# Two heads of the mLSTM scores per TensorE step, gates on 68 rows, and all orders set anew, in a one-core decoder layer

## The reference

```
x = layernorm(x + attention(x))          # 16 heads of 16, score bias by distance, softmax, output projection
x = layernorm(x + mlstm(x, ctx, ctx))    # 4 heads of 64, queries from x, keys and values from ctx
x = layernorm(x + ffn(x))                # 256 -> 1024 (gate, up) -> 256, rows quantised to 8 bits, ternary weights

# mlstm, for each head
ig, fg = concat(x, ctx, ctx) @ gate kernels + biases       # one number per row and head
cs     = cumsum(log_sigmoid(fg));  log_D = cs_i - cs_j + ig_j   (j <= i)
D      = exp(log_D - rowmax(log_D))
C      = (q k^T / 8) * D
h      = C v / (max(|rowsum C|, exp(-rowmax)) + 1e-6), then a norm over each head
```

## Time and profile before

| | us |
|---|---|
| median of 3 executions | 827.5 (827.5 to 833.78) |
| the profiled execution | 828.54 |
| its span, first to last instruction | 826.8 |
| TensorE busy | 698.1 |
| VectorE busy | 640.6 |
| ScalarE busy | 626.0 |
| GpSimd busy | 491.1 |

### The profile page before, as it was taken

How to read it: one execution, slowest core, us unless ns; L and a number is a source line. 1 busy time by engine, 2 the same in 40 slices (tenths; PEclk the granted TensorE clock), 3 DMA queues, 4 the chain that set the end, 5 groups by cost and what they waited for, 6 DMA issues and landing times.

```text
span 826.8 us, 17709 instructions
## 1 busy us (share of the span) xinstructions
PE 698.1 (84%) x5138; PEld 519.6 (63%) x5168; DVE 640.6 (77%) x2437; ACT 626.0 (76%) x1284; POOL 491.1 (59%) x833
## 2 busy tenths in 40 slices
PE   4279888899898989898989898999989898975642
PEld 3257657577675858585858676777758575743411
DVE  3745454888988888888888988988888889876743
ACT  0427674979898988888888989898989888885622
POOL 2536453657677676776675757676776763735232
PEclk8679996999999999999999999999999999989866
DMA  8876734080605060513224160707060601010100
GB/s 257 152 135 78 94 64 79 2 140 2 143 12 141 15 140 15 119 37 95 61 56 100 35 120 4 152 2 146 10 141 14 123 20 53 14 52 14 39 14 13
DMA packets 63177, 59.97 MB, mean 73 GB/s; under 512 B 6437, under 2 KB 62826, under 8 KB 63082
## 3 DMA queue, kind: packets, MB, share of 16 engines
q1 hardware_dynamic: 63082, 58.84, 34.6%
HBM read 29.39 MB, written 4.26 MB: 41 GB/s over the span
## 4 chain that ended last, share of the span: by engine, by line
PE 69%; ACT 8%; DVE 7%; issue 6%; POOL 5%; DMA 3%; SPq 2%; POOLq 0%; DVEq 0%; ACTq 0%
PE pT L604 12%; PE pO L621 8%; PE pC L661 6%; PE pS L588 6%; PE pC L637 3%; PE pA L747 3%; PE pA L637 3%; PE pC L708 2%; PE pB L708 2%; PE pB L574 2%; SPq L296 2%; ACT L1114 2%; PE pA L695 2%; PE pB L757 1%; PE pC L725 1%
## 5 line engine op out<-in xcount | busy, mean ns | idle before, releaser
L1299 DVE CUSTOM_DVE_ANT_0 sc<-pS,bias 128x256 f32<-128x256 f32 x512 | 200.6, 417 | 39.9 <-PE pS L588 37.6
L604 PE MATMUL pT<-ident,sc 128*128 128x128 f32 x1024 | 155.9, 285 | 35.5 <-ACT pr L946 33.1
L946 ACT ACTIVATE pr<-pT 128x512 f32<-128x512 f32 x256 | 149.0, 596 | 19.2 <-PE pT L604 18.8
L604 PEld LDWEIGHTS pT<-ident,sc 128*128 128x128 f32 x1024 | 123.0, 146 | 59.7 <-issue 52.4
L426 POOL TENSOR_SCALAR sc<-sc,mx 128x256 f32<-128x256 f32 x256 | 122.3, 483 | 59.4 <-DVE mx L1299 56.3
L934 ACT ACTIVATE sc<-sc,mx 128x256 f32<-128x256 f32 x256 | 127.8, 512 | 1.1 <-DVE mx L1299 0.9
L588 PE MATMUL pS<-ks,qs 96*128 96x256 bf16 x512 | 97.5, 278 | 5.5 <-DVE mx L1299 5.5
L478 POOL TENSOR_SCALAR_AFFINE_SELECT mb<-mb 128x256 f32<-128x256 f32 x64 | 26.2, 409 | 98.7 <-ACT mb L973 94.2
L621 PE MATMUL pO<-pr,va 128*32 128x256 f32 x1024 | 76.5, 421 | 0.0
L438 POOL TENSOR_SCALAR hq<-h 128x512 bf16<-128x512 f32 x64 | 38.5, 619 | 55.1 <-ACT h L1122 55.1
L588 PEld LDWEIGHTS pS<-ks,qs 96*128 96x128 bf16 x512 | 44.9, 99 | 37.9 <-DVE mx L1299 12.5
(11 more groups left out here) (236 smaller groups left out, 1790.0 us busy)
## 6 DMA issues: line engine op xcount, KB each, us to landing
qs<-parts SPq DMA_DIRECT2D x96, 128.0 KB, 5.4
ks<-parts SPq DMA_DIRECT2D x96, 128.0 KB, 6.3
mb<-mrows SPq DMA_DIRECT2D x16, 512.0 KB, 6.7
xin<-in_x SPq DMA_DIRECT2D x16, 256.0 KB, 2.8
bias<-in_L_attn_pos_bias SPq DMA_DIRECT2D x4, 1024.0 KB, 21.2
xb<-in_x SPq DMA_DIRECT2D x16, 256.0 KB, 7.0
cx<-in_ctx SPq DMA_DIRECT2D x32, 128.0 KB, 2.2
out<-hq SPq DMA_DIRECT2D x16, 256.0 KB, 5.8
```

What stands on the lines that cost most here:

```text
L604: ins = pe.transpose(bank[:, kt * S + t * P:kt * S + t * P + P], sc[:, s % RING, t, kt * P:kt * P + P], ident[:])
L946: act.activation(flat(pr[:, s % RING, :, :]), pT[s % 2][:, :], ACT.Exp, scale=-1.0)\
L1299: dve.tensor_tensor_reduce(out=sc[:, s % RING, t, :], in0=pS[s % 2][:, t * S:t * S + S], in1=bias[:, t, s, ::-1], scale=1.0, scalar=LOW, o ...
```

## The change

1. `mem_scores` takes a pair of heads instead of one. It leases two banks at once, then issues the wide product of head 2*pair (partitions 0 to 63) and of head 2*pair+1 (partitions 64 to 127), then both narrow products in the same turn. There are two such steps for a batch where there were four.
2. The forget gates move from row and column 32 to 64: `gate_w` has 68 columns, `gate_b`, `gt`, `sp` and `am` 68 rows. The gates' products write 68 rows, the exponents are turned with 68 rows.
3. The bodies of all five queues, and the table `uses`, are written in a new order. No step is added or dropped except that four `mem_scores` became two.

The core of the difference:

```diff
-        gate_w = sb("gate_w", [P, 6, 64])
-        gate_b = sb("gate_b", [64, 1])
+        gate_w = sb("gate_w", [P, 6, 64 + XH])
+        gate_b = sb("gate_b", [64 + XH, 1])
...
         uses = [
-            ("cv1", 2, cv_sb, 2), ("qk3", 2, c_sb, 4), ("cv2", 2, cv_sb, 3), ("ott0", 1, att_v, 3),
...
+            ("u1", 3, h_v, 4), ("g2", 3, h_v, 5), ("u2", 3, h_v, 6), ("g3", 3, h_v, 7), ("am", 2, am_a, 2),
+            ("u3", 3, h_v, 8), ("qk0", 2, c_sb, 1), ("qk1", 2, c_sb, 2), ("cv0", 2, cv_sb, 1), ("cv1", 2, cv_sb, 2),
+            ("qk2", 2, c_sb, 3), ("qk3", 2, c_sb, 4), ("cv2", 2, cv_sb, 3), ("ott0", 1, att_v, 3),
...
+            ("k", -2, k_f, 1), ("xqT", 2, xq_sb, 1), ("g0", 2, h_v, 1), ("u0", 2, h_v, 2), ("g1", 2, h_v, 3),
         ]
...
-            def mem_scores(c, hh):
+            def mem_scores(c, pair):
...
-                bank = lease(pe, f"qk{hh}", c)
-                if hh == 0:
+                banks = [lease(pe, f"qk{2 * pair + i}", c) for i in range(2)]
+                if pair == 0:
                     pe.wait_ge(x1T_sb.sem, x1T_sb.at(c, 1))
                     pe.wait_ge(cxT_sb.sem, cxT_sb.at(c, 1))
-                r = slice(64 * (hh % 2), 64 * (hh % 2) + 64)
-                pe.matmul(bank[:, 0:S], cxT[r, hh // 2, 0:P], x1T[r, hh // 2, :], start=True, stop=True)
-                pe.matmul(bank[:, S:S + P], cxT[r, hh // 2, P:S], x1T[r, hh // 2, P:S], start=True, stop=True)\
-                    .then_inc(qk_ps.sem, 1)
+                for i in range(2):
+                    r = slice(64 * i, 64 * i + 64)
+                    pe.matmul(banks[i][:, 0:S], cxT[r, pair, 0:P], x1T[r, pair, :], start=True, stop=True)
+                for i in range(2):
+                    r = slice(64 * i, 64 * i + 64)
+                    pe.matmul(banks[i][:, S:S + P], cxT[r, pair, P:S], x1T[r, pair, P:S], start=True, stop=True)\
+                        .then_inc(qk_ps.sem, 1)
...
-                    pe.matmul(bank[0:64, 0:S], gate_w[:, 2 + kt, :], cxT[:, kt, :], start=(kt == 0), stop=False)
+                    pe.matmul(bank[0:64 + XH, 0:S], gate_w[:, 2 + kt, :], cxT[:, kt, :], start=(kt == 0), stop=False)
...
-                    ins = pe.transpose(bank[:, t * P:t * P + 64], am[:, t * P:t * P + P], ident[0:64, 0:64])
+                    ins = pe.transpose(bank[:, t * P:t * P + 64 + XH], am[:, t * P:t * P + P],
+                                       ident[0:64 + XH, 0:64 + XH])
...
-            r = slice(32, 32 + XH)
+            r = slice(64, 64 + XH)
```

More of the change, by code:

```diff
@@ L542, in body @@
                 mem_residual(f, par)
+                negated(b, 9)
+                rstd(f, 1)
+                negated(b, 10)
+                rstd(e, 2)
                 negated(b, 11)
+                negated(b, 12)
+                negated(b, 13)
+                split_high(n2, 0)
+                output(e)
+                negated(b, 14)
+                split_low(n2, 0)
+                negated(b, 15)
+                split_high(n2, 1)
+                negated(n, 0)
+                negated(n, 1)
+                mem_causal(c, 0)
+                mem_causal(c, 1)
+                negated(n, 2)
+                negated(n, 3)
+                mem_causal(c, 2)
+                split_low(n2, 1)
+                mem_causal(c, 3)
             body(-2)
@@ L827, in body @@
                 n2, n, c, f, e = b + 2, b + 1, b - 1, b - 2, b - 3
+                up_proj(e, 1)
+                gate_proj(e, 2)
+                scores(b, 4, par)
+                up_proj(e, 2)
+                turned(c, 13)
+                gate_proj(e, 3)
+                scores(b, 5, par)
+                turned(c, 14)
+                exponents_turned(f)
+                turned(c, 15)
+                values(c, 2, 1 - par)
+                up_proj(e, 3)
+                mem_scores(f, 0)
+                turned(b, 0)
+                turned(b, 1)
+                scores(b, 6, par)
+                mem_values(f, 0)
+                mem_values(f, 1)
+                scores(b, 7, par)
+                mem_scores(f, 1)
+                values(c, 3, 1 - par)
+                turned(b, 2)
+                scores(b, 8, par)
+                mem_values(f, 2)
+                turned(b, 3)
                 scores(b, 9, par)
[L829 to L832, removed]
                 heads_turned(c, 0)
                 heads_turned(c, 1)
+                turned(b, 4)
+                mem_values(f, 3)
                 scores(b, 10, par)
-                mem_values(f, 3)
-                turned(b, 4)
                 turned(b, 5)
-                inner_turned(e, 0)
+                turned(b, 6)
                 attention_turned(c)
@@ L842, in body @@
                 out_proj(c)
+                inner_turned(e, 0)
                 scores(b, 11, par)
-                turned(b, 6)
                 turned(b, 7)
@@ L1136, in body @@
                 n2, n, c, f, e = b + 2, b + 1, b - 1, b - 2, b - 3
-                mem_late(f, 2)
+                exponentials(b, 1)
                 negated(b, 4)
-                exponentials(b, 1)
-                mem_weights(f, 2)
+                scaled(e, 0)
                 heads_copy(c, 3)
-                mem_late(f, 3)
-                mem_out(f, 0)
-                mem_weights(f, 3)
-                negated(b, 5)
-                scaled(e, 0)
-                mem_out(f, 1)
                 mem_out(f, 2)
                 exponentials(b, 2)
+                negated(b, 5)
+                negated(b, 6)
                 exponentials(b, 3)
-                negated(b, 6)
+                exponentials(b, 4)
                 mem_out(f, 3)
@@ L1204, in body @@
                 mem_weights(c, 1)
+                mem_late(c, 2)
+                mem_weights(c, 2)
+                heads_copy(b, 2)
+                negated(n, 2)
+                mem_out(c, 0)
+                negated(n, 3)
                 exponentials(n, 0)
+                mem_late(c, 3)
+                mem_out(c, 1)
+                mem_weights(c, 3)
             act.wait_ge(v_set.sem, V_BC)
@@ L1560, in body @@
                 biased(b, 10, 0)
+                biased(b, 10, 1)
                 attention_residual(c)
-                biased(b, 10, 1)
                 row_stats(c, 0)
```

277 lines of the change are left out of this document (113 added, 164 removed).

## The result

| | before | after |
|---|---|---|
| median, us | 829.65 (827.5 to 833.78, 4 executions) | 784.36 (781.99 to 787.7, 4 executions) |
| the profiled execution | 828.54 | 782.52 |
| its span | 826.8 | 780.8 |

The ratio is 0.9451, 95% interval 0.9391 to 0.9512: 5.5% faster. The first part of the page of the kernel after answers to rows 1: TensorE's busy time is 50 us less, that of the other three under 6 us less.

The account below looks back on a forecast made before the run. TensorE was taken to bound the middle. Work 37.5, waits 2.6 and half clock 0.9 gave a 41.0 us period instead of 43.81: 30.9 over 11 batches plus 12.5 for start and tail, so 784 us, range 756 to 813.

Parts of the forecast that it names:

- The pairs: Scores on TensorE: two heads run side by side on the row halves, gaining 1.90 us a batch; 0.60 if not.
- 68 rows: Gates on TensorE: 68 columns avoid the layout change, saving 0.34 us at the gates and 0.25 at the turned exponents.
- TensorE's work, 37.5 us: TensorE's work per middle batch falls by 2.5 us, from 40.0 to 37.5.
- The waits, 2.6 us: TensorE's waits per batch: 1.1 at gate_proj(f, 0), 0.8 for feed-forward banks, 0.7 at the pair and first mem_values.
- The half clock, 0.9 us: Half-clock stretches behind TensorE's waits cost between 0 and 1.5 us a batch; 0.9 taken, with some rounding.
- The wait of 2.2 us loses its cause: ScalarE's table loads: from the logarithm's load to the exponential TensorE waits for takes 4.9 us instead of 6.8.
- Start and tail, 12.5 us: The five batches outside the middle each gain 2.5 us of TensorE work, as upper end; nothing as the lower.
- Rival 1: Nothing lost between engines: waits vanish, clock full, ScalarE and VectorE set the period at 38.5; 757 us, chance 0.13.
- rival 2: The pair's row halves run in turn: TensorE's work 1.3 us more, period 42.3; 805 us, chance 0.10.
- Rival 3: Saved time becomes TensorE waits for VectorE and ScalarE, 4.6 us instead of 2.6; period 43.0, 811 us, chance 0.12.
- rival 4: Slower: waits of 2.5 us at gate_proj(f, 0) and 3 at the second pair, both with half clock; 846, chance 0.07.

Follow-up runs that it names:

- a_headwise: Changed kernel with a pair's products issued head by head (wide and narrow of one, then of the other): 785.5 us.
- b_exp11k: Kernel before with one ScalarE step, exponentials(b, 11), moved directly behind the key copy: 827.9 us, ratio 0.995 to the kernel before.
- b_exp11: Kernel before with one ScalarE step, exponentials(b, 11), moved directly behind rows_copy(f): 819.1 us, ratio 0.991 to the kernel before.
- b_pair68: Kernel before, its lists kept, with paired scores at the place of each pair's second head and 68 gate rows: 815.5 us, ratio 0.985.
- a_act: Changed kernel with the key copy on ScalarE cut into eight pieces of 64 columns instead of two of 256: 783.0 us.
- a_rows64: Changed kernel with the gates back on 64 rows and columns, lists and pairs kept: 785.6 us, ratio 0.948 to the kernel before.

## Why the prediction was right, and where its parts were off

The forecast was 784 us and faster; measured were 784.36. The period was put at 41.0 and is 40.97. The terms one by one:

* *The pairs.* Right: side by side, 0.86 us for two heads, and 0.64 more in turn. (What a pair would show was put at 0.95 us, with the step behind it.)
* *68 rows.* Right in the main as TensorE time: 0.24 us at the gates and 0.29 at the turned exponents in the new lists, where 0.34 and 0.25 were put. As a term of the period it was overrated: 0.24 us arrives, and the pairs' 1.3 us arrives as 0.66. I had counted TensorE's savings in full and the waits apart; the waits are made in part of these savings.
* *TensorE's work, 37.5 us.* Mis-sized by 1.0: 40.97 less 2.5 of waits is 38.5. The start value of 40.0 was 0.2 too low, since the 0.3 us at `rows_copy` that I read as a wait is 0.12 and a missing pass. In each middle batch one of two steps, `x1_turned` (above) or `ctx_turned`, starts 0.2 us late without a wait in any view. Steps behind a wait take 0.07 to 0.09 more than without one (0.31 instead of 0.22 at 392.71), and there are five waits in place of two. Some 0.3 us are left unexplained.
* *The waits, 2.6 us.* 2.5, nearly as put, but in other places. `rows_turned` and `gate_proj` together were put at 1.1 and are 1.45; the feed-forward's banks 0.8 against 0.3; the pair and `mem_values` 0.7 against 0.4; one of 0.3 for the row maxima wasn't named.
* *The half clock, 0.9 us.* Wrong: nothing in the middle. It was the one term without a row. It and the 1.0 of TensorE's work cancel; the agreement of the period to 0.03 is luck to that extent.
* *"The wait of 2.2 us loses its cause" through the load's place.* This holds for the new lists, where the 4.9 us were right, but not as the cause: in the old lists moving the load alone brought 9 us or nothing.
* *Start and tail, 12.5 us.* 15.6 from the start and -0.8 from the tail, together more than what had been called the upper end. In the start the clock is part of it (0.85 before, 0.95 after, in one execution each), and the start was 164 to 176 us long, to the third batch's heads, over the profiled executions with the new lists, so this isn't settled to better than some microseconds.

The total agrees more closely than its parts: the span fell by 46.0 us, not 43.4, and the profiled execution happened to lie 1.8 us under its kernel's median, where the one before had lain near its own. That 784 and 784.36 differ by 0.4 is luck, too.

Rival 1 is out (waits of 2.5 us, period far above 38.5), rival 2 too. Rival 3 had the right idea of where saved time goes, since about half of what each part saved went into waits, but not its size: 2.5 us in place of 4.6. Of rival 4 nothing came: no wait formed at the second pair, and the first `mem_values` waits 0.4 us.

## What to carry to other kernels

Before pricing a saving on the busiest engine, find in the chain of waits which part of the period that engine closes; only there does a microsecond count, and half of what was saved here went into waits. A list that has several short waits in place of one long one can gain without waiting less: here the longest fell from 2.2 to 0.8 us, the sum stayed, and no half clock was left. It isn't enough to cut the wait in two: 0.96 and 1.25 us close together brought half clock again. Where three engines are nearly as busy as each other, one moved step shows the next late one: four such tries brought 9 us at the most, the new lists 26. And before a wait is read off a view, count the passes of its product: a missing one looks like 0.2 us of waiting, and a delay of 0.2 us can be hidden behind the product before.

## What the runs showed of the hardware

* Products on the two row halves run side by side even when the list has both products of one half first (0.02 us between the wide ones' starts in `a_headwise`). Issuing the halves in turn, as the change does, isn't needed for it.
* Two waits of 0.96 and 1.25 us with 0.6 us of work between were followed by half clock in 10 of 11 batches (`b_exp11k`), one of 1.7 us in 2 of 11 (`b_exp11`), one of 2.2 us in 9 of 11 (before) and 7 of 11 (`b_pair68`), waits of 0.8 us and less in none (the kernel after).
* Eight activations of 64 columns took 0.68 us more than two of 256 (1.57 against 0.89, `a_act`).
* Leaving 64 columns for 68 took 0.24 us off the gates and 0.29 off the turned exponents (`a_rows64` against the kernel after).
